# Two weights, the x scales and the o quantisation change engines, with new orders, in a fused decoder layer

## What is computed

```python
def _bitlinear(x, w):
    xn = _rmsnorm(x)
    s = 127.0 / clip(max(abs(xn), axis=-1), 1e-05)
    xq = clip(round(xn * s), -128.0, 127.0) / s
    ws = 1.0 / clip(mean(abs(w)), 1e-05)
    wq = clip(round(w * ws), -1.0, 1.0) / ws
    return einsum('bld,od->blo', xq, wq)

i = _bitlinear(x, Wi); f = sigmoid(_bitlinear(x, Wf))
i = silu(i) * (1.0 - f)
h = scan over the tokens of a batch: h = f * h_before + i
o = _rmsnorm(_bitlinear(x, Wg)) * g_norm_weight * (h * sigmoid(h))
x = layernorm(x + _bitlinear(o, Wo))                          # 1

# every token goes to one of four experts, by its id; all three weights of an expert are ctx[e]
y = einsum('bsf,df->bsd', silu(x @ ctx[e].T) * (x @ ctx[e].T), ctx[e])
x = layernorm(x + y)                                          # 2

x = layernorm(x + einsum('btd,rde->bte', x, factors) / sqrt(8) + bias)   # 3, eight 512x512 factors
```

## Time and profile before

| | us |
|---|---|
| Runs of the kernel, three | 343.01, 343.08, 340.66 |
| Median | 343.01 |
| The profiled execution | 342.06 |
| Its span in the trace | 340.3 |
| TensorE busy in the span | 278.1 (82%) |
| ScalarE | 229.6 (67%) |
| VectorE | 226.3 (66%) |
| GpSimd | 190.8 (56%) |

### The profile page before, as it was taken

One profiled execution on the slowest core, in us unless ns is written; L12 is line 12 of the kernel. 1 busy time (PEld: TensorE's weight loads), 2 busy tenths in 40 slices (PEclk: granted clock), 3 DMA queues, 4 the chain that ended last, 5 costly groups with the idle time before them and its releaser, 6 DMA issues.

```text
span 340.3 us, 5734 instructions
## 1 busy us (share of the span) xinstructions
PE 278.1 (82%) x1505; PEld 211.9 (62%) x1518; DVE 226.3 (66%) x488; ACT 229.6 (67%) x456; POOL 190.8 (56%) x381
## 2 busy tenths in 40 slices
PE   1376646484879899999999998998999999999760
PEld 1253414252557678787778876676888888887540
DVE  2789999999987879968677696454543434543310
ACT  4687789889678769986887686476555644554530
POOL 2536765858637748865565856547444444454442
PEclk9999989879799999999999999999999999999975
DMA  7999981987593782013003002205111111000000
GB/s 233 387 388 387 225 196 62 185 153 143 130 227 79 115 179 65 1 62 126 0 33 141 17 15 111 62 7 186 56 40 56 62 66 62 33 26 29 4 6 0
DMA packets 17406, 37.02 MB, mean 109 GB/s; under 512 B 1503, under 2 KB 1631, under 8 KB 17376
## 3 DMA queue, kind: packets, MB, share of 16 engines
q0 software_dynamic: 6496, 15.74, 19.6%
q1 hardware_dynamic: 10880, 20.92, 19.2%
HBM read 26.68 MB, written 10.76 MB: 110 GB/s over the span
## 4 chain that ended last, share of the span: by engine, by line
PE 62%; ACT 9%; issue 5%; DVE 5%; DMA 2%; POOL 2%; ACTq 0%; POOLq 0%; DVEq 0%; SPq 0%
PE bank_y L1455 5%; PE bank_z L1455 5%; PE bank_y L1456 5%; PE bank_z L1456 5%; PE bank_z L1459 5%; PE bank_y L1459 5%; PE bank_m L1455 4%; PE bank_m L1456 4%; PE bank_m L1459 4%; PE bank_tr L1424 3%; PE bank_c L1357 2%; PE bank_q L1424 2%; PE bank_a L1357 1%; PE bank_b L1357 1%; DMA sorted_rows<-r,place 1%
## 5 line engine op out<-in xcount | busy, mean ns | idle before, releaser
L312 POOL TENSOR_SCALAR n_v<-n_dev 128x1 f32<-128x1 f32 (+1 forms) x46 | 8.8, 192 | 52.2 <-ACT x L644 26.7
L1455 PE MATMUL bank_y<-c_hi,h_hi 128*128 x76 | 31.8, 418 | 1.8 <-ACT h_hi L612 1.4
L996 DVE TENSOR_TENSOR act_z<-bank_z,act_z 128x512 f32<-128x512 f32 x19 | 13.1, 689 | 30.1 <-ACT act_z L626 30.1
L1455 PE MATMUL bank_m<-f_hi,m_hi 128*128 128x512 f32 x76 | 32.1, 423 | 0.8 <-ACT m_hi L612 0.8
L353 POOL TENSOR_TENSOR x<-x,bias_b 128x512 f32<-128x512 f32 x19 | 24.6, 1293 | 14.5 <-PE bank_q L1424 14.5
L1455 PE MATMUL bank_z<-c_hi,a_hi 128*128 x76 | 30.4, 400 | 2.8 <-ACT a_hi L612 1.5
L1456 PE MATMUL bank_m<-f_lo,m_hi 128*128 128x512 f32 x76 | 30.8, 405 | 0.0
L1456 PE MATMUL bank_y<-c_lo,h_hi 128*128 x76 | 30.1, 396 | 0.0
L1456 PE MATMUL bank_z<-c_lo,a_hi 128*128 x76 | 30.1, 395 | 0.0
L612 ACT ACTIVATE h_hi<-bank_tr 128x512 fp32r<-128x512 f32 x19 | 11.3, 596 | 26.7 <-PE bank_tr L1424 26.7
L313 POOL TENSOR_TENSOR n_d<-n_v,minus_half 128x1 f32<-128x1 f32 (+1 forms) x46 | 27.1, 588 | 3.8
(11 more groups left out here) (205 smaller groups left out, 848.7 us busy)
## 6 DMA issues: line engine op xcount, KB each, us to landing
f_sum<-in_factors POOLq DMA_DIRECT2D x7, 1024.0 KB
rows<-sorted_rows SPq DMA_DIRECT2D x19, 256.5 KB, 2.9
xs<-in_x SPq DMA_DIRECT2D x8, 512.0 KB, 7.6
c_stage<-in_ctx_t SPq DMA_DIRECT2D x4, 1024.0 KB, 14.3
...
```

Of the source, the lines that this page charges most:

```text
L996: v.tensor_tensor(act_z[:], bank_z[:], act_z[:], ALU.mult).then_inc(s.hid, 1)
L1455: t.matmul(bank[:], hi[:, c, :], w_hi(c), start=(c == 0), stop=False)
```

## The change

Three pieces of work change engine:

- Weights 2 (W_G) and 3 (W_O): ScalarE scales and rounds in one pass (scale_weights), VectorE clips in one pass (clip_weights), instead of two passes on VectorE.
- The scale of x for groups 2 to 7: five instructions on GpSimd (scale_x_pool), with a power of -1 instead of the reciprocal. Groups 0 and 1 stay on VectorE.
- quantise_o for pairs 0 to 2 goes to GpSimd; VectorE's version is removed.

And the lists of GpSimd, ScalarE, VectorE and TensorE are written in another order; SP's stays. What the prediction speaks of:

```diff
+                def scale_x_pool(g):
+                    i = g % 2
+                    pool.wait_ge(s.xch, XCH * (g + 1))
+                    pool.wait_ge(s.mxx, GT * g + GT)
+                    link(pool.tensor_tensor(x_mr[:], x_max[:, i, :], x_r[:, i, :], ALU.mult), s.xsc)
+                    after(pool, s.mcb, g - 1)
+                    pool.tensor_scalar(x_mc[:, i, :], x_mr[:], GUARD, None, ALU.max).then_inc(s.x_mc, 1)
+                    pool.wait_ge(s.x_mc, g + 1)
+                    link(pool.tensor_tensor(x_rc[:, i, :], x_mc[:, i, :], minus_one[:], ALU.pow), s.xsc)
+                    link(pool.tensor_scalar(x_mr[:], x_rc[:, i, :], QMAX, None, ALU.mult), s.xsc)
+                    pool.tensor_tensor(x_q[:, i, :], x_mr[:], x_r[:, i, :], ALU.mult).then_inc(s.xq_s, 1)
...
+                def scale_weights(m):
+                    act.wait_ge(s.wscale, 2 * m + 2)
+                    a.activation(w_stage[:, m, :], w_stage[:, m, :], ACT.Copy, bias=MAGIC, scale=w_scale[:, m:m + 1]
+                                 ).then_inc(s.wround_act, 1)
...
-                def quantise_o(p):
-                    dve.wait_ge(s.oq_s, p + 1)
-                    dve.wait_ge(s.sqo, GT * p + GT)
-                    for j in range(GT):
-                        tile = o_tok[:, p % 2, j, :]
-                        v.tensor_scalar(tile, tile, o_q[:, j:j + 1], HALF_MAGIC, ALU.mult, ALU.add).then_inc(s.qo, 1)
...
+                def clip_weights(m):
+                    dve.wait_ge(s.wround_act, m - W_I)
+                    v.tensor_scalar(w_stage[:, m, :], w_stage[:, m, :], MAGIC + 1.0, MAGIC - 1.0, ALU.min, ALU.max
+                                    ).then_inc(s.wclip, 1)
```

TensorE, before the loop and in a turn:

```diff
                 silu_h_by_token(3)
+                transpose_a(0)
                 project_f(4)
-                transpose_a(0)
+                up(0)
                 project_i(4)
-                up(0)
+                transpose_h(0)
                 project_g(4)
-                transpose_h(0)
...
                 up(1)
+                project_back(3)
+                transpose_h(1)
                 pe.wait_ge(s.oqt, 4)
                 transpose_m(0)
-                transpose_h(1)
-                project_back(3)
+                down(1)
                 transpose_a(2)
-                down(1)
                 up(2)
...
                     project_g(g)
+                    down(n - 1)
                     if is_group(g + 1):
                         pe.wait_ge(s.tml, n - 2)
                         transpose_x(g + 1)
-                    down(n - 1)
+                    transpose_a(n)
+                    mix(n - 3)
                     pe.wait_ge(s.xqt, min(g + 2, N_GROUPS))
                     transpose_m(n - 2)
                     if is_group(g + 1):
                         spread_max(g + 1)
-                    transpose_a(n)
-                    mix(n - 3)
                     up(n)
                     pe.wait_ge(s.tml, n - 1)
                     transpose_o(p)
                     mix(n - 2)
                     transpose_h(n)
-                    pe.wait_ge(s.oqt, p + 1)
-                    transpose_m(n - 1)
                     project_back(p)
                     transpose_a(n + 1)
                     down(n)
+                    pe.wait_ge(s.oqt, p + 1)
+                    transpose_m(n - 1)
                     up(n + 1)
```

443 lines of the change are left out of this document (223 added, 220 removed).

## The result

The changed kernel took 346.44 us (median of 14 runs; before took 340.88, also of 14, on the same chip). The ratio to before is 1.0153, with a 95% interval of 1.0122 to 1.0185: 1.5% slower, where 0.5% faster was predicted (341.3 against 343.01, the median of the first three runs of before). The profiled execution took 348.22 us with a span of 346.0 us; that of before took 342.06 with 340.3.

The account below looks back on a forecast made before the run. VectorE was taken to bound the start (busy 74.43 of 77 us). Entry -2.1, before the turns -0.2, in them -0.2, hand-over +0.8 sum to -1.7 us: from 343.01 to 341.3, range 337.5 to 345.5.

Parts of the forecast that it names:

- the walk: Start: new lists followed instruction by instruction to up(1) at 104.9 us, a gain of 2.8, cut to 2.1.
- The 0.8 of the hand-over: Hand-over: add_bias(6) ahead of store(5) delays scale_o(7) and the rows of slot 11, costing 0.8 us.
- VectorE's relief: Start, 20 to 97 us: moved work takes 8.6 us off VectorE, clip_weights included, leaving 65.8 us busy.
- second rival: Start: stretched scale_x_pool calls of 3.3 us make scatter_rows(2) 5.6 us late, kernel slower at 346.9 us; chance 0.17.
- No engine is the clear bound any more: Start: budget of VectorE 65.8, ScalarE 68.8, GpSimd 59.7 of 77 us, so waits between engines now show.
- GpSimd sets it: Start: project_back(0) at 48.7 us is set by GpSimd, scale_o(0) beginning at 42.5 and quantise_o(0) ending at 46.8.
- The 0.7 us set aside: Start: taken off the walk's gain for seven or eight handoffs of VectorE and ScalarE, at 0.1 each.
- The turns: Three steady turns: seams of 0.1 to 0.2 us close, a gain of 0.2 us in all three.
- Before the turns: Entry after up(1): project_back(3) fills TensorE's 0.98 us stand before transpose_h(1), net gain 0.2 us.
- the predicted sign: Hand-over: scale_o(7) at least a microsecond behind output(7, 1)'s squares, with TensorE standing before transpose_o(7).

Follow-up runs that it names:

- e14: The changed kernel with scale_x(2) to (5) and quantise_o(0) to (2) back on VectorE, new orders kept: 1.0201 of before.
- e2: The kernel before with quantise_o(0) to (2) on GpSimd, each directly behind its scale_o: 1.0036 of before.
- e9: The changed kernel with VectorE's rescale_f(2, 1) moved directly behind rescale_f(2, 0), as in before: 1.0237 of before.
- e7: All engines' lists of the start from the kernel before, turns and hand-over from the changed kernel: 1.0047 of before.
- e13: The kernel before, its orders kept, with weights 2 and 3 scaled on ScalarE, quantise_o(0) to (2) and scale_x_pool(2) to (7) on GpSimd: 1.0202 of before.
- e16: e7 with store(5) of the last turn moved from ahead of scale_o(7) to behind quantise_o(7): 1.0014 of before.
- e18: All engines' lists of the start from the changed kernel, turns and hand-over from the kernel before: 1.0083 of before.

## Why the prediction was wrong

The step that failed is the walk through the start. It had up(1) at 104.9 us, a gain of 2.8, cut to 2.1; it came at 113.46, 5.76 later than before. The terms below say where. The 0.8 of the hand-over was too small as well, and its wait was another than predicted.

**VectorE's relief**: near in size, in part by luck. Predicted 65.8 us busy, measured 66.14. But the window ends at a fixed 97 us, and the later kernel had not yet done three rescales, low_a(0) and one half of output(3, 1) by then, 3.4 us that the window of before holds. In return other work of VectorE got longer, which the prediction named beside its second rival and had at nothing in its sum: the 16 scans that go on from a state (h_ch<-f_ch,h_ch,i_ch, 128x256) took 812 ns on average where they took 735 in before; the 16 that begin a batch did not (672 and 692). One pair in after, and GpSimd's quantise_o(2) beside it:

```profile
86.33 2.21 DVE L959 TENSOR_TENSOR_SCAN h_ch<-f_ch,h_ch,i_ch 128x256 f32<-128x256 f32 x2
```

```profile
85.98 2.02 POOL L306 TENSOR_SCALAR o_tok<-o_tok,o_q 128x512 f32<-128x512 f32 x2
```

That it comes with quantise_o is shown by runs. In before and the nine edits that keep quantise_o(0) to (2) on VectorE the mean is 734 to 737 ns, e14 with the new orders (735) among them. In the changed kernel and the nine edits that have it on GpSimd it is 761 to 876, e2 with nothing else moved (831) among them.

scale_weights took 2.01 and 1.99 us (1.9 predicted). "No engine is the clear bound any more" was right as well, and so was what the prediction says next, that the waits of the engines for each other now show; the next step, to walk it and take 2.1 us from it, failed.

**The walk**, its excess over the forecast cut at TensorE's steps. From 20 us to project_back(0): 52.34 against 48.7, 3.6 us late. "GpSimd sets it" was right and its durations were wrong: the prediction says itself that the walk gives GpSimd "its undisturbed times". scale_o(0) began at 43.76 (walk 42.5), and with quantise_o(0) took 6.7 us where the walk gave 4.3. In the windowed groups above the o tile takes 1195 ns where pairs 3 to 7 took 784. So 1.3 us are the late beginning (scale_x_pool(2) took 3.0 us for 1.9) and 2.4 are scale_o(0) and quantise_o(0). I had bounded scale_x_pool by the stretched rows and taken the low end; for scale_o and quantise_o I had put no stretch at all, though the rows of o_rc are scale_o's own. The 0.7 us set aside was for handoffs.

This stretch can be seen in e9. GpSimd's clip of scale_o(1), on 128x2 elements, and what VectorE did meanwhile:

```profile
60.53 3.35 POOL L293 TENSOR_SCALAR o_mc<-o_mf 128x2 f32<-128x2 f32 x1
```

```profile
60.69 1.90 DVE L1044 TENSOR_TENSOR c_lo<-c_stage,c_hi 128x512 fp32r<-128x512 f32 x3
62.50 0.69 DVE L951 SCALAR_TENSOR_TENSOR i_ch<-t_ch,i_ch 128x512 f32<-128x512 f32 x1
63.10 0.69 DVE L1044 TENSOR_TENSOR c_lo<-c_stage,c_hi 128x512 fp32r<-128x512 f32 x1
```

An instruction of 0.2 us took 3.35 and ended 0.1 us after VectorE's last of five without a gap. The Trainium skill (SBUF — State Buffer, Who interferes with whom) states that a VectorE instruction with two SBUF inputs contends with a GpSimd instruction that reads SBUF; all five have two, and the trace agrees. VectorE's rows here stay at 0.68 to 0.69. The stretch was kept for a rival, and there for the new work alone. By the rows above it belonged into the main sum, for scale_o and quantise_o too; as a term with a range, since scale_x_pool(3) to (5) took 1.9 us each, undisturbed.

**From project_back(0) to (1)**: 20.77 us against 18.8. The walk had ScalarE's queue as the bound. It was rescale_f(2, 1), which the new list of VectorE has behind output(1, .), both max_o and quantise_x(3); e9 shows that this wait is the list's own. Behind it project_g(2) ran at the lower level of TensorE's clock, 3.4 us in place of some 1.8 at the higher one, with transpose_x(3) queued behind; the walk took the durations of before. I had also missed that residual_1(1) can't write before scatter_rows(0) has landed: 1.25 us in after, 4.59 in e9.

**From project_back(1) to (2)**: 17.80 against 16.9, with no single wait that explains it; and **from there to up(1)**: 22.55 against 20.5. Of these last 2.05 us, 0.37 are residual_1(2) (2.64 us behind the product's start, before 2.27), 0.77 scatter_rows(2), which waited for scale_x_pool(5) though norm_1(2) was done at 100.11, and 0.95 lie between transpose_a(1) and up(1), 1.08 of them idle with nothing named by the profile. The four pieces are 3.6, 2.0, 0.9 and 2.05 us, 8.6 in all, which takes the walk's 104.9 to the measured 113.46. Against before, and not the walk, they are 2.95, 0.52, 0.24 and 2.05 us, 5.76 in all: the loss itself sits in the first piece and the last, and the middle two are mostly gains that didn't come.

**The second rival** gave 346.9 us, near the 346.44 measured, by luck and not by its own way. It is 1.1% above the 343.01 that it counts from, and the changed kernel is 1.5% above the runs beside it. It has every scale_x_pool at 3.3 us and all of it on scatter_rows(2). Only scale_x_pool(2) took 3.0; (3) to (5) took 1.9 each. The scatter was 4.84 us late because project_back(2) was already 3.7 late. Its ground, that GpSimd's instructions are stretched in the start, was seen, but mostly in other calls than it named.

**The turns**: -0.2 predicted, +0.2 in the profile, no difference. **Before the turns**: no gain of 0.2; from up(1) to the turn it is 13.17 us in both.

**The hand-over**: the place was right, the wait was not, and the size was off. scale_o(7) began late as predicted (5.52 us behind the fourth silu_h_by_token, before 4.55). But the predicted sign, TensorE standing before transpose_o(7), isn't in the trace: it stood before transpose_a(9), one step ahead, for the rows of slot 9, and the late o tiles were hidden behind that. A wait for these rows wasn't in the prediction at all. The cost was 1.26 us in the profile and 1.6 (0.6 to 2.6) in e7's ratio, for 0.8 predicted.

What stays open. Whether VectorE's list or GpSimd's load weighs more in the start can't be said as a share: e13 and e14 each cost 2.0% and together, with the orders made for the moves, 1.5%. What the lower granted clock of the start costs by itself wasn't run. Why the load of slot 9's rows took 4.28 us in after and 4.20 in e7 from its issue, 3.6 in e16 and 2.8 in e18, isn't settled; in e16's one profile moving the store goes with 0.6 of it. The stretch of GpSimd's instructions wasn't switched off in a run, so its share of the loss is argued, not shown.
